# A recurrence's closing addition on GpSimd, and the turned maxima read by ScalarE

## The chip, the cores and the metric

One core of one Trainium2 chip runs the whole program. The time is device microseconds of one launch. The kernel before took 487.45 us, the median of three runs (486.83 to 490.58).

## The reference, cut to what matters

x is 2 x 1024 tokens of 128 channels. A layer norm gives xn, and the output is x plus two branches of xn.

```
xn  = layernorm(x)
out = x + attn_ref(xn) + ffn_ref(xn)

attn_ref(x):                       # a WKV recurrence over the 1024 tokens, per channel
    h = LN(x); k, v, r = mixes of h and h shifted, times w_tk, w_tv, w_tr
    y = wkv(decay, first, k, v)    # running max, running sum, running weighted sum
    x1 = x + sigmoid(r) * y
    h2 = LN(x1); ck, cr = mixes of h2 and h2 shifted
    return x1 + sigmoid(cr @ w_cr) * (square(relu(ck @ w_ck)) @ w_cv)

ffn_ref(x):                        # 16 heads of width 8, weights from a gated sum of experts
    q, k, v = effective weights applied to x
    ctx = softmax(q k^T, over keys) v
    return ctx @ w_o + b_o
```

The last line of `attn_ref` has the addition that the change moves. The maxima are those of the softmax in `ffn_ref`: each query's largest score over its 1024 keys.

## The kernel before, in words

**Attention.** There are 32 attention rows (2 batches x 16 heads), taken as 16 pairs of heads. For each pair the scores are made twice. First with queries on the partitions, only to find the row maxima: 32 "places" of 128 queries x 512 keys, each one bf16 matmul (`fill_place`, L1256) into one of three PSUM banks in turn (5, 6, 7), which VectorE reduces to one negated maximum per query (`read_place`, L1080). The two halves of a row are combined at the pair's last place (L1084). A 33rd place, `TURN_PLACE`, is a TensorE transpose of these 128 x 16 maxima (L1250) into 16 x 128 in the next bank of the same three; VectorE copies it to `max_rows` in SBUF (L1075). GpSimd splits it into three bf16 parts (`split_max`, L616 to L622), and SyncE writes these as three more rows of the queries (`place_max`, L448, six DMAs).

Then the scores are made again with keys on the partitions, maxima subtracted by those extra rows (`scores`, L1330), into banks 0 to 3. ScalarE takes the exponential of 2 x 512 columns at a time (`exps`, L887), and TensorE multiplies them by the values into bank 4 (`values`, L1341). A pair has 8 steps of 128 keys, each with two such exponentials.

**The order.** The program is unrolled over 16 pairs x 8 steps. Every engine has its own list in program order, and semaphores join them. In each step TensorE issues: two places of a later pair, the step's scores (half h = 0, then h = 1), two more places, the transposed maxima if it is their turn, the values of the step before, then perhaps a product of the recurrence. VectorE reads the step's four places in order, then the recurrence's operations of that step (`branch`). ScalarE does the two exponentials, then its own `branch`. A place may be filled once the place three fills earlier has been read; the semaphore `a_read` counts all reads, the transposed ones too.

**The recurrence.** The other branch is spread over the same steps, in four quarters of 256 tokens. A quarter lasts four pairs, 32 steps, and step t of a quarter has fixed work: windows are copied by GpSimd at t = 1, three scans run on VectorE at t = 2, 6 and 12, ScalarE has a Relu and an Exp at each of t = 9 to 12, the second layer norm and mixes come at t = 17 to 21, and the products at t = 22 to 29 (`PRODUCT_STEP`). At t = 29 VectorE multiplies the product by the gate into `gx` (L1061) and adds `x1` into `RT` (L1063), with `rt_ready`. GpSimd's copy of the quarter's ends at the next t = 1 (L639) waits for `rt_ready`, and so does TensorE's last stage. The lists of GpSimd add the output bias to x at t = 30 (L694).

The transposed maxima of the next pair come at the fourth step after a pair's start: t = 4, 12, 20 and 28 of a quarter, 15 times in the loop, and once more before the loop, where ScalarE copies twelve `parts` (L776) of the second batch's queries and keys.

The places for a pair run about one and a half pairs ahead, so in the last quarter they end before t = 20.

Of the kernel before, what the change touches and what calls it, by code (L numbers as in the profile page):

```python
# [6 lines left out]
P = 128  # L7
TILES = B * T // P
CHUNK = 512
CHUNKS = B * T // CHUNK  # L10
HEADS, HD = 16, 8
EXPERTS, RANK, GATE_H = 8, 16, 32
PAIRS = B * HEADS // 2
KEY_TILES = T // P
PARTS = 3
# [7 lines left out]
TURN_PLACE = 4  # L23
SPLIT_STEP = 4
A_PLACES = 33
PV_BANK, A_BANK = 4, 5
# [4 lines left out]
SETS = 4  # L31
QUARTERS, QT = 4, 256
# [15 lines left out]
def build(nc, x, cols, mats, rows, gw1, gb1, gw2, gb2, out):  # L48
    F32, BF16 = mybir.dt.float32, mybir.dt.bfloat16
    ALU, ACT, AX = mybir.AluOpType, mybir.ActivationFunctionType, mybir.AxisListType  # L50

    ctx = ExitStack()
    with ctx:
# [3 lines left out]
        def sem(name):  # L57
            return ctx.enter_context(nc.semaphore(name))
# [16 lines left out]
        RT = sb("RT", [P, B, T])  # L75
# [70 lines left out]
        gated = sem("gated")  # L146
        relu_ready = sem("relu_ready")
        a_read = sem("a_read")
        max_parts_ready = sem("max_parts_ready")
        ctx_copied = sem("ctx_copied")  # L150
        moe_in = sem("moe_in")
# [139 lines left out]
        def bank(i):  # L291
            return banks[:, i, :]
# [46 lines left out]
        def exists(it, pair, k):  # L339


            n = it * SETS + pair
            if not isinstance(n, int):
                return True
            return 1 <= n <= PAIRS if k == TURN_PLACE else n < PAIRS

        def a_count(it, pair, k):

            n = it * SETS + pair
            if isinstance(n, int) and n == 0:  # L350
                return k if k < TURN_PLACE else k - 1
            if isinstance(n, int) and n == PAIRS:
                return PAIRS * A_PLACES - 1
            return n * A_PLACES + k - 1

        turns, place_turns = [], []
        for t in range(SETS * KEY_TILES):  # L360
            here = []
# [16 lines left out]
        def turn_bank(turn):  # L378
            return bank(A_BANK + (turn + A_PLACES + LEAD - 1) % 3)
# [7 lines left out]
        def wait_for_bank(pe, it, turn):  # L387

            if turn < 3:
                pe.wait_ge(a_read, a_count(it, *turns[turn]) - 1)  # L390
                return
            turn -= 3
            while isinstance(turns[turn], tuple) and not exists(it, *turns[turn]):
                turn -= 3
            if isinstance(turns[turn], tuple):
                pe.wait_ge(a_read, a_count(it, *turns[turn]) + 1)
            else:
                taken, of, n = taken_by[turns[turn]]
                pe.wait_ge(taken, it * of + n)
# [11 lines left out]
        def first(p):  # L411
            return isinstance(p, int) and p == 0
# [118 lines left out]
        def _(pool):  # L531
# [77 lines left out]
            def split_max(p, s, it=0, pair=0):  # L609
                rows_, res_ = max_rows[:, s % 2, :], max_res[:, s % 2, :]  # L610
                m0, m1, m2 = (max_parts[:, s % 2, i, :] for i in range(PARTS))
                transposed = a_count(it, pair + 1, TURN_PLACE) + 1
                pool.wait_ge(a_read, transposed)
                if not (isinstance(p, int) and p < 2):
                    pool.wait_ge(b_ready, (p - 1) * 16 + 1)
                g.tensor_tensor(m0, rows_, zero_rows[:, :], ALU.add).then_inc(max_part, 1)  # L616
                pool.wait_ge(max_part, p * 3 + 1)
                g.tensor_tensor(res_, rows_, m0, ALU.subtract).then_inc(max_part, 1)
                pool.wait_ge(max_part, p * 3 + 2)
                g.tensor_tensor(m1, res_, zero_rows[:, :], ALU.add).then_inc(max_part, 1)  # L620
                pool.wait_ge(max_part, p * 3 + 3)
                g.tensor_tensor(m2, res_, m1, ALU.subtract).then_inc(max_parts_ready, 1)  # L622
# [10 lines left out]
            def branch(t, q):  # L633
# [56 lines left out]
                        mix(q, i, h2[:, :, 0:QT])  # L690
                if t == 30:

                    here = x_sb[:, 4 * q:4 * q + 4, :]
                    g.tensor_tensor(here, here, vb_ob[:, 1:2, :].to_broadcast([P, 4, C]), ALU.add  # L694
                                    ).then_inc(xob_ready, 1)
# [25 lines left out]
        def _(act):  # L721
# [61 lines left out]
            for u, n in enumerate(CHUNK_ORDER):  # L783
                act.wait_ge(h_transposed, u + 1)
                a.activation(hT[:, n // 2, 1 + CHUNK * (n % 2):1 + CHUNK * (n % 2 + 1)], bank(h_bank(u)), ACT.Identity,
                             bias=col("ln1_b"), scale=col("ln1_g")).then_inc(h_ready, 1)

            def keep_v(n):

                act.wait_ge(v_ps, n + 1)  # L790
                here = V[:, 8 * (n // 2):8 * (n // 2) + 8, 4 * (n % 2):4 * (n % 2) + 4, :]
                a.copy(here.rearrange("p r k w -> p k r w"), bank(v_bank(n)).rearrange(
                    "p (k r w) -> p k r w", k=CHUNK // P, w=2 * HD)).then_inc(v_read, 1)
# [29 lines left out]
            keep_v(3)  # L823
            keep_kvr(2)
            keep_kvr(3)
            for i in range(PARTS):
                for j in range(CHUNKS):
                    part(j, 1, i)

# [2 lines left out]
            def branch(t, q):  # L832
# [47 lines left out]
                if t == 28:  # L880
                    act.wait_ge(cr_step, q * 2 + 2)
                    a.activation(ecr[:, :, :], ecr[:, :, :], ACT.Exp, scale=-1.0).then_inc(cr_ready, 1)

            def exps(p, step):
                for h in range(2):
                    act.wait_ge(b_ready, p * 16 + 2 * step + h + 1)
                    a.activation(probs[:, (2 * step + h) % 4, :, :], banks[:, 2 * h:2 * h + 2, :],  # L887
                                 ACT.Exp).then_inc(b_read, 1)
# [5 lines left out]

            def head(p, j, it):
                exps(p, 0)
                if not first(p):
                    copy_ctx(p - 1, (j - 1) % SETS, it * 2 + (j - 1) // 2)
                branch(j * KEY_TILES, it)

            def rest(p, j, it):
                for step in range(1, KEY_TILES):
                    exps(p, step)
                    branch(j * KEY_TILES + step, it)

            def tail():
# [14 lines left out]
        def _(dve):  # L921
# [119 lines left out]
            def branch(t, q):  # L1041

                if t == 2:

                    dve.wait_ge(carried, q + 1)
                    dve.wait_ge(windows, q * 4 + 1)
                    scan(q, run_max, k_q, col("decay"), ALU.max, ALU.add, run_max_ready)
                if t == 6:

                    dve.wait_ge(decays_ready, q * 2 + 2)  # L1050
                    scan(q, run_sum, w1, w2, ALU.mult, ALU.add, sum_ready)
                if t == 12:
                    dve.wait_ge(ev_ready, q + 1)
                    scan(q, run_acc, lo_u, ev, ALU.mult, ALU.add, acc_ready)
                if t == PRODUCT_STEP["mean"]:
                    dve.wait_ge(mean2_ps, q + 1)
                    v.tensor_tensor(flat(xc2), flat(x1), product_bank("mean"), ALU.subtract).then_inc(centred2, 1)
                if t == PRODUCT_STEP["cv"]:
                    dve.wait_ge(cr_ready, q + 1)
                    dve.wait_ge(cv_ps, q + 1)  # L1060
                    v.tensor_tensor(flat(gx), product_bank("cv"), flat(ecr), ALU.mult).then_inc(gated, 1)  # L1061
                    dve.wait_ge(gated, q + 1)
                    v.tensor_tensor(RT[:, :, bass.ds(q * QT, QT)], x1[:, :, :], gx[:, :, :], ALU.add  # L1063
                    ).then_inc(rt_ready, 1)

            def read_place(it, pair, k, src):

                if not exists(it, pair, k):
                    return
                n, s, pair_n = a_count(it, pair, k), pair % 2, it * SETS + pair  # L1070
                if k == TURN_PLACE:
                    if not isinstance(pair_n, int) or pair_n >= 2:
                        dve.wait_ge(max_parts_ready, pair_n - 1)
                    dve.wait_ge(a_ready, n + 1)
                    v.tensor_copy(max_rows[:, (s + 1) % 2, :], src[0:2 * KEY_TILES, 0:P]).then_inc(a_read, 1)  # L1075
                    return
                e, c, h = place_of(k)
                u = 16 * e + 2 * c + h
                dve.wait_ge(a_ready, n + 1)
                v.tensor_reduce(neg_half[:, s, u:u + 1], src, axis=AX.X, op=ALU.max, negate=True  # L1080
                ).then_inc(a_read, 1)
                if k == A_PLACES - 1:
                    dve.wait_ge(a_read, n + 1)
                    v.tensor_reduce(neg_max[:, s, :], neg_half[:, s, :].rearrange("p (c h) -> p c h", h=2),  # L1084
                                    axis=AX.X, op=ALU.min).then_inc(half_combined, 1)

# [35 lines left out]
        def _(pe):  # L1122
# [155 lines left out]
            for pair, k in places(0, A_PLACES + LEAD):  # L1278
                if not exists(0, pair, k):
                    continue  # L1280
                n = a_count(0, pair, k)
                if n >= 3:
                    pe.wait_ge(a_read, n - 2)
                fill_place(0, pair, k, bank(A_BANK + n % 3))
                between(n)
            for j in range(CHUNKS):
# [148 lines left out]
```

## Time and profile before

| | before |
|---|---|
| median of three runs | 487.45 us |
| the profiled execution's own time | 487.07 us |
| its span, first to last instruction | 485.3 us |
| TensorE matmul busy | 443.6 us, 91% |
| VectorE busy | 372.2 us, 77% |
| ScalarE busy | 354.2 us, 73% |
| GpSimd busy | 180.9 us, 37% |
| chain that ended last, by engine | PE 58%, DVE 23%, ACT 13% |
| granted TensorE clock, mean | 0.981 |

The loop's first scores start at 76.8 us and its last exponential at 463.1 us. In the trace's names PE is TensorE, PEld its weight loads, DVE VectorE, ACT ScalarE, POOL GpSimd, SPq SyncE's DMA queue. A row of the timeline merges equal instructions (x4) and gives their common stretch; in square brackets stands the idle time of the engine before it and what ended it.

### The profile page before, as it was taken

The page shows a single profiled execution, that of the slowest core. Times are in us where ns is not written, and L with a number is a line of the kernel's source. Part 1 is how long each engine was busy: PE and PEld are TensorE (multiplying, and loading weights), DVE is VectorE, ACT ScalarE, POOL GpSimd, SP SyncE. Part 2 cuts the span into 40 slices and gives each one's busy share as a digit, 9 for nine tenths or more (in the row PEclk, how much of TensorE's full clock was granted, in tenths as well). Part 3 has the DMA queues.
Part 4 walks back from the last instruction along what each step waited for, and adds up shares of the span by engine and source line. Part 5 has one row for each costly group of instructions (what it writes and reads, how often), then busy time and mean ns, then how long its engine had stood idle before and what let it go on. Part 6 is the DMA issues. An engine that isn't in the chain of part 4 may idle for free.

```text
span 485.3 us, 8374 instructions
## 1 busy us (share of the span) xinstructions
PE 443.6 (91%) x3156; PEld 147.9 (30%) x3158; DVE 372.2 (77%) x670; ACT 354.2 (73%) x453; POOL 180.9 (37%) x236
## 2 busy tenths in 40 slices
PE   2886998999999999999999999999999999989996
PEld 2751322222223322222232222222322222222275
DVE  7543997999988689999877899998778999940113
ACT  2266773689888666898986668989875689899651
POOL 7048940414651414146514141375141313751200
PEclk9999995999999999999999999999999999999998
DMA  6004421132323223323232232332322321102132
GB/s 219 11 8 52 61 23 23 12 54 26 57 22 59 19 45 33 51 28 56 23 58 22 28 51 50 30 52 26 57 24 22 55 45 12 28 9 80 31 105 91
DMA packets 46684, 21.35 MB, mean 44 GB/s; under 512 B 37556, under 2 KB 37684, under 8 KB 46644
## 3 DMA queue, kind: packets, MB, share of 16 engines
q1 hardware_dynamic: 45824, 20.13, 25.5%
q10 hardware_dynamic: 820, 0.68, 0.4%
q8 instruction: 25, 0.41, 0.3%
q14 instruction: 15, 0.12, 0.1%
HBM read 4.88 MB, written 5.24 MB: 21 GB/s over the span
## 4 chain that ended last, share of the span: by engine, by line
PE 58%; DVE 23%; ACT 13%; issue 2%; SPq 2%; DMA 1%; DVEq 0%
PE banks L1341 17%; DVE neg_half L1080 15%; PE banks L1330 12%; PE banks L1256 11%; ACT probs L887 9%; PE banks L1302 8%; DVE run L1038 3%; PE banks L1231 2%; PE banks L1164 2%; PE banks L1388 2%; PE banks L1383 2%; PE banks L1129 1%; ACT work L846 1%; SPq L431 1%; ACT work L844 1%
## 5 line engine op out<-in xcount | busy, mean ns | idle before, releaser
L1080 DVE TENSOR_REDUCE neg_half<-banks 128x1 f32<-128x512 f32 x512 | 319.1, 682 | 39.1 <-PE banks L1256 37.4
L887 ACT ACTIVATE probs<-banks 128x1024 f32<-128x1024 f32 x256 | 247.7, 1022 | 66.3 <-PE banks L1330 63.6
L1341 PE MATMUL banks<-probs,v_op 128*32 128x512 f32 x1024 | 137.2, 608 | 0.4 <-ACT probs L887 0.4
L1256 PE MATMUL banks<-k_main,q_main 64*128 64x512 bf16 x512 | 120.3, 388 | 15.0 <-DVE neg_half L1080 12.1
L1330 PE MATMUL banks<-q_main,k_main 64*128 64x512 bf16 x512 | 101.2, 382 | 5.0 <-ACT probs L887 3.7
L1330 PE MATMUL banks<-q_tail,k_tail 35*128 35x512 bf16 x512 | 100.9, 381 | 0.0
L1256 PEld LDWEIGHTS banks<-k_main,q_main 64*128 64x128 bf16 x512 | 36.0, 94 | 168.1 <-DVE neg_half L1080 145.2
L1330 PEld LDWEIGHTS banks<-q_main,k_main 64*128 64x128 bf16 x512 | 26.0, 95 | 44.5 <-ACT probs L887 32.1
L1330 PEld LDWEIGHTS banks<-q_tail,k_tail 35*128 35x128 bf16 x512 | 26.6, 95 | 23.7 <-issue 1.1
L1061 DVE TENSOR_TENSOR rec<-banks,quarter_in 128x512 f32<-128x512 f32 x4 | 2.8, 690 | 37.8 <-PE banks L1302 37.8
L700 POOL TENSOR_TENSOR work<-work 128x512 f32<-128x512 f32 x12 | 12.5, 1040 | 49.8 <-ACT work L872 49.8
L1341 PEld LDWEIGHTS banks<-probs,v_op 128*32 128x32 f32 x1024 | 20.2, 108 | 33.1 <-issue 30.0
L616 POOL TENSOR_TENSOR max_parts<-max_rows,zero_rows 16x128 bf16<-16x128 f32 x16 | 11.2, 701 | 31.9 <-DVE max_rows L1075 31.9
L649 POOL TENSOR_TENSOR xn_tok<-run 128x512 f32<-128x512 f32 x4 | 4.2, 1039 | 49.7 <-DVE run L1038 49.7
L1302 PE MATMUL banks<-xn_tok,mat_sb 128*32 128x512 f32 x160 | 20.8, 592 | 0.0
L654 POOL TENSOR_TENSOR work<-work 128x512 f32<-128x512 f32 x4 | 5.1, 1276 | 41.8 <-ACT work L840 41.8
L1129 PE MATMUL banks<-ones_c,xn_tok 128*128 128x1 f32 x32 | 7.2, 353 | 8.8 <-DVE xn_tok L929 8.8
L658 POOL TENSOR_TENSOR hT<-work,quarter_in 128x512 f32<-128x512 f32 x4 | 5.1, 1272 | 18.7 <-ACT work L846 18.7
L1231 PE MATMUL banks<-work,mat_sb 128*128 128x512 f32 x16 | 8.9, 639 | 3.1 <-POOL work L594 2.8
L872 ACT ACTIVATE work<-banks 128x512 f32<-128x512 f32 x12 | 7.2, 601 | 5.7 <-PE banks L1302 5.7
L1302 PE MATMUL banks<-work,mat_sb 128*32 128x512 f32 x96 | 11.0, 592 | 0.0
L776 ACT ACTIVATE parts<-banks,qb_s 128x512 bf16<-128x512 f32 x9 | 6.1, 686 | 6.6 <-PE banks L1164 5.7
(164 smaller groups left out, 429.4 us busy)
## 6 DMA issues: line engine op xcount, KB each, us to landing
ctx_dram<-ctx_sb SPq DMA_DIRECT2D x16, 256.0 KB, 2.0
q_main<-parts SPq DMA_DIRECT2D x64, 48.0 KB
k_main<-parts SPq DMA_DIRECT2D x64, 48.0 KB
parts<-ctx_dram SPq DMA_DIRECT2D x8, 256.0 KB, 4.4
mat_sb<-in_mats_dram SPq DMA_DIRECT2D x2, 768.0 KB, 5.3
q_tail<-max_parts SPq DMA_DIRECT2D x96, 2.0 KB
q_main<-parts SPq DMA_DIRECT2D x32, 32.0 KB
k_main<-parts SPq DMA_DIRECT2D x32, 32.0 KB
```

The costliest lines, as they stand in the source:

```text
L616: g.tensor_tensor(m0, rows_, zero_rows[:, :], ALU.add).then_inc(max_part, 1)
L700: g.tensor_tensor(kk[i][:, :, :], kk[i][:, :, :], kk[i][:, :, :], ALU.mult).then_inc(kk_ready, 1)
L887: a.activation(probs[:, (2 * step + h) % 4, :, :], banks[:, 2 * h:2 * h + 2, :], ACT.Exp).then_inc(b_read, 1)
L1038: v.tensor_tensor_scan(out_[:, b, 1:], c0[:, b, :], data1, out_[:, b, 0:1], op0, op1).then_inc(done, 1)
L1080: v.tensor_reduce(neg_half[:, s, u:u + 1], src, axis=AX.X, op=ALU.max, negate=True).then_inc(a_read, 1)
L1129: last = mm(banks[:, 4, 24 + b:25 + b], xn_tok[:, i, :], ones_c[:, :], start=(k == 0), stop=(k == TILES // B - 1))
L1164: mm(bank(j), w_eff[:, t, b, :], columns_of(xnT, n), start=True, stop=True).then_inc(left_ps[j], 1)
L1231: mm(bank(kvr_bank(m)), mat("t" + "kvr"[m % 3]), mix_slot[m % MIX_SLOTS], start=True, stop=True).then_inc(kvr_ps, 1)
L1256: mm(dst, q_main[HALF * e:HALF * (e + 1), s, P * c:P * c + P], k_main[HALF * e:HALF * (e + 1), s, CHUNK * h:CHUNK * h + CHUNK], start=True ...
L1302: last = mm(dst[g:g + 32, :], weights[:, g:g + 32], moving, start=start, stop=stop)
L1330: last = mm(bank(2 * h + e), k_rows[HALF * e:HALF * e + used, at, P * step:P * step + P], q_rows[HALF * e:HALF * e + used, at, CHUNK * h:C ...
L1341: last = mm(banks[g:g + 32, PV_BANK, :], v_op[:, s % 2, step, e, :], probs[:, (2 * step + h) % 4, e, :], start=(step == 0), stop=(step == ...
```

## The change

The addition into `RT` leaves VectorE's step 29 for the head of GpSimd's step 30. The copy of the transposed maxima leaves VectorE's `read_place` for ScalarE: `copy_turned`, called behind the step's two exponentials and ahead of ScalarE's `branch` of that step. The reads of that place get a semaphore of their own, `turn_read`, and `read_of` says for each fill which semaphore and count stand for its read. Before the loop ScalarE copies the first transposed maxima between the first four and the last eight `parts`.

```diff
+        turn_read = sem("turn_read")
...
+        fill_seq = [(n, k) for n in range(PAIRS + 1) for k in range(A_PLACES) if exists(0, n, k)]
+
+        def read_of(at):
+
+            n, k = fill_seq[at]
+            turned = sum(place[1] == TURN_PLACE for place in fill_seq[:at + 1])
+            return (turn_read, turned) if k == TURN_PLACE else (a_read, at + 1 - turned)
...
             def split_max(p, s, it=0, pair=0):
-                transposed = a_count(it, pair + 1, TURN_PLACE) + 1
-                pool.wait_ge(a_read, transposed)
+                pool.wait_ge(turn_read, p + 1)
...
                 if t == 30:
 
+                    pool.wait_ge(gated, q + 1)
+                    g.tensor_tensor(RT[:, :, bass.ds(q * QT, QT)], x1[:, :, :], gx[:, :, :], ALU.add
+                                    ).then_inc(rt_ready, 1)
                     here = x_sb[:, 4 * q:4 * q + 4, :]
...
+            def copy_turned(n, src):
+
+                if n >= 2:
+                    act.wait_ge(max_parts_ready, n - 1)
+                act.wait_ge(a_ready, fill_seq.index((n, TURN_PLACE)) + 1)
+                a.copy(max_rows[:, (n + 1) % 2, :], src[0:2 * KEY_TILES, 0:P]).then_inc(turn_read, 1)
...
-            for i in range(PARTS):
+            for j in range(CHUNKS):
+                part(j, 1, 0)
+            copy_turned(1, bank(A_BANK + fill_seq.index((1, TURN_PLACE)) % 3))
+            for i in (1, 2):
                 for j in range(CHUNKS):
                     part(j, 1, i)
...
+            def turned_step(p, j, it, step):
+
+                for turn in (*place_turns[j * KEY_TILES + step][0], *place_turns[j * KEY_TILES + step][1]):
+                    pair, k = turns[turn]
+                    if k == TURN_PLACE and exists(it, pair, k):
+                        copy_turned(it * SETS + pair, turn_bank(turn))
...
                     exps(p, step)
+                    turned_step(p, j, it, step)
                     branch(j * KEY_TILES + step, it)
...
                     v.tensor_tensor(flat(gx), product_bank("cv"), flat(ecr), ALU.mult).then_inc(gated, 1)
-                    dve.wait_ge(gated, q + 1)
-                    v.tensor_tensor(RT[:, :, bass.ds(q * QT, QT)], x1[:, :, :], gx[:, :, :], ALU.add
-                    ).then_inc(rt_ready, 1)
...
                 if k == TURN_PLACE:
-                    if not isinstance(pair_n, int) or pair_n >= 2:
-                        dve.wait_ge(max_parts_ready, pair_n - 1)
-                    dve.wait_ge(a_ready, n + 1)
-                    v.tensor_copy(max_rows[:, (s + 1) % 2, :], src[0:2 * KEY_TILES, 0:P]).then_inc(a_read, 1)
                     return
```

TensorE's waits for a free bank (`wait_for_bank`, and the loop ahead of the main one) name `read_of` of the same fill as before.

## Rows read from the trace of the kernel before

**Rows 1.** Stretches by `windows`: busy us (instructions) by engine, then PEclk, DMA share, GB/s.
```profile
74.00:85.00 11.00, 9.74 (x41) 2.79 (x42) 7.78 (x14) 3.88 (x4) 0.00 (x0) 0.53 0.22 25
167.30:264.90 97.60, 93.36 (x736) 26.81 (x732) 86.51 (x146) 77.64 (x94) 35.91 (x44) 1.00 0.28 39
```

**Rows 2.** Groups of instructions by shape: busy us, mean ns, idle before.
```profile
L893 ACT COPY ctx_sb<-banks 128x512 f32<-128x512 f32 x16 | 9.5, 592 | 1.2 <-PE banks L1341 1.2
...
L694 POOL TENSOR_TENSOR x_sb<-x_sb,vb_ob 128x512 f32<-128x512 f32 x4 | 5.1, 1269 | 0.0
...
L1063 DVE TENSOR_TENSOR RT<-work,rec 128x512 f32<-128x512 f32 x4 | 2.8, 691 | 0.1
...
L769 ACT ACTIVATE mat_sb<-mat_sb 128x128 f32<-128x128 f32 x1 | 0.3, 312 | 0.0
```

**Rows 3.** Chain of waits (start, length, what) about step 29 of the second quarter.
```profile
268.42 0.70 DVE rec L1061
...
269.15 0.69 DVE RT L1063
...
270.50 0.39 PE banks L1256
```

**Rows 4.** VectorE's timeline (start, length, instruction) at step 17 of that quarter.
```profile
228.39 0.69 DVE L1057 TENSOR_TENSOR work<-work,banks 128x512 f32<-128x512 f32 x1 [0.76 <-PE banks L1302]
228.99 2.48 DVE L1080 TENSOR_REDUCE neg_half<-banks 128x1 f32<-128x512 f32 x4
```

**Rows 5.** GpSimd's timeline, step 2 of the third quarter.
```profile
283.96 1.04 POOL L649 TENSOR_TENSOR xn_tok<-run 128x512 f32<-128x512 f32 x1 [11.62 <-DVE run L1038]
```

**Rows 6.** VectorE's row reduction, line 1080, one line's view: ns min/median/max.
```profile
L1080 DVE TENSOR_REDUCE neg_half<-banks x512: 653/680/693, 42.2 to 429.4; 128x1 f32<-128x512 f32 x171
```

**Rows 7.** VectorE's timeline behind the copy of step 4.
```profile
191.74 0.69 DVE L1080 TENSOR_REDUCE neg_half<-banks 128x1 f32<-128x512 f32 x1 [0.30 <-PE banks L1256]
```

**Rows 8.** ScalarE's timeline, the exponentials of steps 5 and 29.
```profile
192.18 1.02 ACT L887 ACTIVATE probs<-banks 128x1024 f32<-128x1024 f32 x1 [1.16 <-PE banks L1330]
...
263.16 1.94 ACT L887 ACTIVATE probs<-banks 128x1024 f32<-128x1024 f32 x2 [0.51 <-PE banks L1330]
```

**Rows 9.** Chain of waits at step 12, and ScalarE's copy at step 8.
```profile
202.77 0.48 ACT ctx_sb L893
...
213.82 0.19 DVE max_rows L1075
```

**Rows 10.** ScalarE's timeline, the exponentials of step 13.
```profile
215.89 1.92 ACT L887 ACTIVATE probs<-banks 128x1024 f32<-128x1024 f32 x2
```

**Rows 11.** TensorE's weight loads and matmuls at step 14.
```profile
217.86 0.10 PEld L1330 LDWEIGHTS banks<-q_main,k_main 64*128 64x128 bf16 x2 [0.28 <-ACT probs L887]
...
217.92 0.38 PE L1330 MATMUL banks<-q_main,k_main 64*128 64x512 bf16 x2
...
218.35 0.46 PE L1256 MATMUL banks<-k_main,q_main 64*128 64x512 bf16 x2
```

**Rows 12.** TensorE's weight loads at step 22.
```profile
240.84 0.10 PEld L1330 LDWEIGHTS banks<-q_main,k_main 64*128 64x128 bf16 x2 [0.54 <-ACT probs L887]
```

**Rows 13.** The path of the maxima from step 12 to 16: GpSimd, SyncE's queue, TensorE.
```profile
214.08 1.47 POOL L616 TENSOR_TENSOR max_parts<-max_rows,zero_rows 16x128 bf16<-16x128 f32 x1 [2.95 <-DVE max_rows L1075]
...
L616 POOL TENSOR_TENSOR max_parts<-max_rows,zero_rows x16: 442/444/1473, 69.6 to 432.2; 16x128 bf16<-16x128 f32 x16
...
217.09 4.00 SPq L448 DMA_DIRECT2D q_tail<-max_parts  x6
...
222.46 0.38 PE L1330 MATMUL banks<-q_main,k_main 64*128 64x512 bf16 x2
```

**Rows 14.** Before the loop: chain of waits, and two matmuls of TensorE's timeline.
```profile
69.23 0.19 DVE max_rows L1075
...
68.09 0.28 PE L1250 MATMUL banks<-ident,neg_max 128*16 128x128 f32 x1
...
69.65 0.39 PE L1170 MATMUL banks<-parts,neg_ident 128*128 128x512 bf16 x1
```

More of the change, by code:

```diff
@@ L389, in wait_for_bank @@
             if turn < 3:
-                pe.wait_ge(a_read, a_count(it, *turns[turn]) - 1)
+                pe.wait_ge(*read_of(a_count(it, *turns[turn]) - 2))
                 return
@@ L395, in wait_for_bank @@
             if isinstance(turns[turn], tuple):
-                pe.wait_ge(a_read, a_count(it, *turns[turn]) + 1)
+                pe.wait_ge(*read_of(a_count(it, *turns[turn])))
             else:
@@ L896, in head @@
                 exps(p, 0)
+                turned_step(p, j, it, 0)
                 if not first(p):
@@ L1082, in read_place @@
                 if k == A_PLACES - 1:
-                    dve.wait_ge(a_read, n + 1)
+                    dve.wait_ge(*read_of(n))
                     v.tensor_reduce(neg_max[:, s, :], neg_half[:, s, :].rearrange("p (c h) -> p c h", h=2),
@@ L1282, in _ @@
                 if n >= 3:
-                    pe.wait_ge(a_read, n - 2)
+                    pe.wait_ge(*read_of(n - 3))
                 fill_place(0, pair, k, bank(A_BANK + n % 3))
```

## The prediction

> **What bounds the kernel.** I began with the stretches [rows 1]. Quarters repeat every 97.6 us at full clock. In one TensorE is busy 93.4 us, VectorE 86.5, ScalarE 77.6, GpSimd 35.9. No engine is full, so each moved operation must be followed in the chain of waits. In most steps it goes through TensorE alone. It goes through VectorE where the recurrence puts something between the reads of places, and through ScalarE where a branch stands between exponentials. An edit counts only there.
>
> **The addition into RT, off VectorE.** The multiply by the gate starts at 268.42, the addition at 269.15, and TensorE's next place, waiting for the first read behind them, starts at 270.50 [rows 3]: all on the chain. Without it that read follows the multiply directly. A tensor_tensor from PSUM is followed by a read after 0.60 [rows 4], so the read starts at 269.02 and not at 269.15 + 0.60 = 269.75: 0.73 us sooner. VectorE's reads of that step and the next two stand back to back, so they carry it to the next quarter. Three quarters have places behind step 29; in the last one there is nothing left to read and TensorE's last stage comes later. Gain 3 x 0.73 = 2.19 us.
>
> **The addition, on GpSimd.** GpSimd takes 1.27 us for two full operands [rows 2], against 0.69 on VectorE. Its step 30 now waits for `gated`; behind it are queued the bias addition (another 1.27), the quarter's ends and four windows. What hides them: GpSimd sits idle 11.6 us before step 2's scan is done [rows 5], and the scan needs only the ends and the first window. In the last quarter the bias addition is needed by VectorE's last stage, after the exponentials have ended. I price it at nothing; without the cover it would cost 1.27 a quarter. The Trainium skill ("SBUF — State Buffer", Terms, shared port pair) speaks against the move: the two engines lock each other out of a shared port for a whole instruction. What that would do to the reads here is priced among the rivals.
>
> **The copies, off VectorE.** There are 16, each worth 0.19 in the chain [rows 9]. At steps 4, 20 and 28 (11 of the 15 in the loop) VectorE then idles for TensorE's next place 0.30 at one [rows 7], the others alike (behind the last quarter's step 20 no read follows at all): no gain. At step 12 (4 times) the copy stands before the scan on the chain [rows 9]: 0.19 each. Before the loop it also stands on it [rows 14]: 0.19 once.
>
> **The copies, on ScalarE.** No row shows a 16x128 copy there. Durations: 592 ns for 128x512 out of PSUM, 312 for 128x128 in SBUF [rows 2]. What counts is what it holds up: the 592 ns copy takes 0.48 in the chain [rows 9], 0.11 less, as the next starts before it ends. From 0.31 this makes 0.20, which I take, since the size is the same. Bounds: 0.08 (0.19, VectorE's pitch for it, less 0.11) and 0.59, a whole large copy with nothing overlapped. Call it C. The Trainium skill ("VectorE: DVE Perf Modes", the TRN2 errata) has another: 172 cycles plus one per element at 1.2 GHz for ScalarE from PSUM, so an estimated 0.25 long and 0.14 held up; the rule gives 0.57 for the 512 copy, near the row's 0.592. By it the sum below would be 1.7 us faster than before.
>
> Where is C exposed?
> - Steps 4 and 28: ScalarE idles 1.16 and 0.51 before the next exponentials [rows 8]. Hidden. TensorE needs the bank only a step later.
> - Step 12: ScalarE has no gap. The exponentials of step 13 run 215.89 to 217.81 and TensorE's load for the second half of step 14 waits for them until 217.86 [rows 10, 11]; the matmul at 217.92 is just not late. Pushed by C they end at 217.81 + C, the matmul comes 0.05 to 0.07 later: 218.08 with C = 0.20, so 0.16 late. The two places behind it take 0.46 instead of 0.38 [rows 11], since the second waits 0.08 for the read of this step's first place; a late first half absorbs that. Net C - 0.11 = +0.09, which replaces the 0.19 gained at VectorE: if C were 0 the step would give back -0.19.
> - Step 20: no gap at ScalarE either, its layer-norm and mix operations run end to end with exponentials, and TensorE's load at step 22 already waits for them [rows 12]. C in full, +0.20.
> - Before the loop: four `parts` now wait for the transpose at 68.09 (0.28) and C: the first then ends at 68.37 + 0.05 + 0.20 + 0.69 = 69.31, and TensorE takes it at 69.65 [rows 14]. Hidden by 0.34.
>
> Both exposed steps come in all four quarters.
>
> **The new wait and the maxima's path.** GpSimd's split at step 12 starts 0.9 us later than before (behind 214.6 instead of 213.8), but its first operation took 1.47 us there beside VectorE's scan, against a median of 0.44 [rows 13], and the scan is then nearly over: it ends at about the same time. By the Trainium skill's port rule, above, the row is as it should be, since the scan reads SBUF. The six DMAs are issued until 221.09 and step 16 scores at 222.46 [rows 13]: 1.4 us in which they must land. This is the tightest point; I cost it at nothing, and bound it at +-0.3 a quarter.
>
> **The sum**, against the profiled execution's own 487.07 us (span 485.3 and 1.8 around it):
> - RT: -2.19
> - before the loop: -0.19
> - step 12: 4 x 0.09 = +0.36
> - step 20: 4 x 0.20 = +0.80
>
> Together -1.22: 485.85. The median of the three runs lies 0.38 above this execution, so I forecast **486.2 us**, 0.25% faster. As a formula, with all else as above: -2.82 + 8C. Net zero is at C = 0.35.
>
> **The rivals.**
> - *ScalarE pays more* (0.14). The mechanism is the copy's length at steps 12 and 20. If its wait and its semaphore leave nothing overlapped, C passes 0.35 and the kernel is slower; at C = 0.59 it is +1.90, 489.35. For it: ScalarE has no gap at either place. Against: every ScalarE row that I read overlaps by 0.1.
> - *RT's gain doesn't arrive* (0.09). Something else, the fill of `gated`'s bank or the exponentials, ends that wait. Then -0.63 + 1.60 (8C) = about +1.0: 488.4. Against it: ScalarE idles there, and the second place of step 30 waits for nothing but the read.
> - *GpSimd's addition blocks VectorE's reads* (0.03). Instead of -0.73 it would be +0.54 a quarter: 3 x 1.27 on top of the sum, 490.0. Against it: all 512 reads took 653 to 693 ns [rows 6], whatever GpSimd did beside them.
> - *The clock's low stretch moves* (0.08). From 74 to 85 us the granted clock was 0.53 [rows 1], near the 1.2 GHz level, after TensorE had been waiting on reads; all else in the loop ran at 2.4 GHz. The edit shifts the reads just ahead of it by 0.2 us. In such 11 us the matmul work of 9.74 us would take about half at full clock, less what waits anyway: I take 3.3 us either way, 482.9 or 489.5, 0.04 each.
> - *The maxima land late at step 16* (0.04): 4 x 0.3 on top, 487.4.
> - The forecast case has 0.62. That the change doesn't do what it says I can leave out: both moves are plain edits of the lists.
>
> **Range and chances.** The forecast case by itself spans C from 0.08 to 0.3, 485.1 to 487.0, and runs of this kernel differ by 0.6 to 3.1 us. The range 484.6 to 489.0 takes in the rivals but the clock's two ends and the blocked reads. Within 1% (4.9 us, about what a measurement tells from no change) lie all cases but tails of the clock: faster by over 1% 0.03, within 1% 0.94, slower 0.03.
>
> **What would show it.** `RT` on GpSimd right behind the gate multiply, 1.27 long, and TensorE's place of step 30 at 0.73 less after that multiply's start (1.35 instead of 2.08). A quarter of 97.6 - 0.73 + 0.09 + 0.20 = 97.2 us. ScalarE's copy at 0.25 to 0.31 long; the load at step 14 waiting longer than 0.28, the load at step 22 longer than 0.54. No idle TensorE before step 16. It would be wrong if quarters lengthened, if GpSimd's first split operation at step 12 still took 1.4 us, or if the low clock lasted other than about 10 us.

## The result and the profile after

| | before | after |
|---|---|---|
| median of 20 runs each, side by side | 488.95 us | 485.87 us |
| lowest and highest run | 485.51 to 491.61 | 482.72 to 489.30 |
| profiled execution's own time, span | 487.07, 485.3 | 484.93, 483.2 |
| a quarter (step 29's last product to the next) | 97.61, 97.60 | 96.82, 96.83 |

After to before is 0.9948, 95% interval 0.9923 to 0.9972: faster by 0.5%, 1.4 to 3.8 us. The forecast was 486.2, 1.22 us less than before. The spans of the two profiled executions differ by 2.1 us. By the starts of the step-29 multiply, the changed kernel is 0.22 behind in the first quarter (171.04 to 170.82), and then 0.56, 1.33 and 2.12 ahead (457.68 to 459.80): three times 0.77 to 0.79, less 0.22. Single runs of either kernel differ by more than the change brings, so what follows is read by quarters, which repeat to 0.03 us.

The chain of waits of the changed kernel about step 29 of the second quarter (start, length, what):

```profile
267.86 0.69 DVE rec L1091
268.56 0.61 DVE neg_half L1103
...
269.21 0.39 PE banks L1279
```

Against [rows 3]: the read now follows the gate multiply by 0.70 and TensorE's place starts 1.35 after that multiply, where it was 2.08. That is the forecast number, 1.35.

GpSimd's timeline at the same place, and then VectorE's scan of step 2 that it must not delay:

```profile
268.63 1.27 POOL L702 TENSOR_TENSOR RT<-work,rec 128x512 f32<-128x512 f32 x1 [4.90 <-DVE rec L1091]
...
271.23 0.62 POOL L650 COPY quarter_in<-kept_k 128x512 f32<-128x512 f32 x1
```
```profile
281.20 1.38 DVE L1068 TENSOR_TENSOR_SCAN run<-quarter_in,run,col_sb 128x256 f32<-128x256 f32 x2
```

The addition takes 1.27 and the first window starts at 271.23, 10 us before the scan, which waits for nothing (no bracket).

ScalarE's timeline at steps 12 and 20:

```profile
212.28 1.92 ACT L915 ACTIVATE probs<-banks 128x1024 f32<-128x1024 f32 x2
214.09 0.24 ACT L804 COPY max_rows<-banks 16x128 f32<-16x128 f32 x1
214.24 0.72 ACT L865 ACTIVATE hT<-work,neg_first 128x512 f32<-128x512 f32 x1
```
```profile
236.95 0.24 ACT L804 COPY max_rows<-banks 16x128 f32<-16x128 f32 x1
237.09 1.33 ACT L888 ACTIVATE xn_tok<-xn_tok,col_sb 128x512 f32<-128x512 f32 x2
```

The copy is 0.24 long and holds up what is behind it by 0.15 (214.09 to 214.24) and 0.14 (236.95 to 237.09). I had taken 0.20 from the nearest rows; the Trainium skill's figure ("VectorE: DVE Perf Modes", the TRN2 errata) gave an estimated 0.25 and 0.14, and the trace agrees with it.

TensorE's timeline at step 17, before and after:

```profile
226.21 1.07 PE L1341 MATMUL banks<-probs,v_op 128*32 128x512 f32 x8
227.26 1.06 PE L1302 MATMUL banks<-work,mean_w 128*32 128x512 f32 x8
```
```profile
225.71 1.06 PE L1364 MATMUL banks<-probs,v_op 128*32 128x512 f32 x8
226.59 1.06 PE L1325 MATMUL banks<-work,mean_w 128*32 128x512 f32 x8
```

Here is what I had not foreseen. The product of the means started 1.05 us after the values ahead of it; now it does so after 0.88, which is what the eight matmuls of values ahead of it take when nothing waits. So before the change it was held for 0.17. What held it shows in the timelines of TensorE's weight loads, GpSimd and VectorE (its row is that of the stretch from 226 to 227 us), first before, then after:

```profile
227.23 0.19 PEld L1302 LDWEIGHTS banks<-work,mean_w 128*32 128x32 f32 x8 [0.87 <-DVE neg_half L1080]
...
225.85 1.27 POOL L676 TENSOR_TENSOR work<-hT,quarter_in 128x512 f32<-128x512 f32 x1
...
225.75 1.88 DVE L1080 TENSOR_REDUCE neg_half<-banks 128x1 f32<-128x512 f32 x3
```
```profile
226.56 0.19 PEld L1325 LDWEIGHTS banks<-work,mean_w 128*32 128x32 f32 x8 [0.69 <-DVE neg_half L1103]
...
225.17 1.28 POOL L684 TENSOR_TENSOR work<-hT,quarter_in 128x512 f32<-128x512 f32 x1
```

The product waits for two things: its PSUM bank, which is free once VectorE has read the second of the step's four places, and its operand `x1`, which GpSimd's last addition of step 16 writes (`x1_ready`). The bracket names VectorE. But the read of that second place, the first of the three in the row, starts at 225.75 and takes 0.68, so the bank was free 0.8 us before the load of 227.23. `x1` was ready at 227.12, 0.11 before it. In every quarter of all ten traces the product's first load starts 0.11 to 0.12 after `x1` is written. So it was GpSimd's `x1` that held TensorE, not a bank.

TensorE's weight loads at steps 21 and 22 of the changed kernel, against [rows 12]:

```profile
240.28 0.10 PEld L1353 LDWEIGHTS banks<-q_main,k_main 64*128 64x128 bf16 x2 [0.65 <-ACT probs L915]
```

The wait for the exponentials grew from 0.54 to 0.65: step 20's copy costs 0.11. The same wait at step 14 grew from 0.28 to 0.60, as the prediction's signs had it.

### The profile page after: what moved, and what is told of

Its sections match the earlier page's. It is cut to its first block, busy times and chain, and to the rows that moved or that the text cites. A ratio compares the mean times of both kernels' runs of the same rounds, so it can differ in the third digit from the quotient of the medians.

```text
span 483.2 us, 8374 instructions
## 1 busy us (share of the span) xinstructions
PE 444.6 (92%) x3156; PEld 147.4 (31%) x3158; DVE 367.2 (76%) x650; ACT 356.0 (74%) x469; POOL 182.1 (38%) x240
## 3 DMA queue, kind: packets, MB, share of 16 engines
q1 hardware_dynamic: 45824, 20.13, 25.5%
## 4 chain that ended last, share of the span: by engine, by line
PE 54%; ACT 22%; DVE 18%; issue 2%; SPq 2%; DMA 1%; DVEq 0%
PE banks L1364 15%; ACT probs L915 14%; DVE neg_half L1103 12%; PE banks L1353 11%; PE banks L1279 10%; PE banks L1325 8%; PE banks L1254 2%; DVE run L1068 2%; PE banks L1411 2%; PE banks L1406 2%; PE banks L1187 1%; ACT work L867 1%; ACT work L865 1%; PE banks L1152 1%; ACT xn_tok L888 1%
## 5 line engine op out<-in xcount | busy, mean ns | idle before, releaser
L624 POOL TENSOR_TENSOR max_parts<-max_rows,zero_rows 16x128 bf16<-16x128 f32 x16 | 7.1, 446 | 36.0 <-ACT max_rows L804 36.0
L1254 PE MATMUL banks<-work,mat_sb 128*128 128x512 f32 x16 | 10.7, 775 | 2.8 <-POOL work L603 2.8
L702 POOL TENSOR_TENSOR RT<-work,rec 128x512 f32<-128x512 f32 x4 | 5.1, 1273 | 21.4 <-DVE rec L1091 21.4
L666 POOL TENSOR_TENSOR hT<-work,quarter_in 128x512 f32<-128x512 f32 x4 | 5.1, 1273 | 18.7 <-ACT work L867 18.7
```

The source lines that it names most:

```text
L1254: mm(bank(kvr_bank(m)), mat("t" + "kvr"[m % 3]), mix_slot[m % MIX_SLOTS], start=True, stop=True).then_inc(kvr_ps, 1)
```

## The experiments

A quarter is the time between the starts of step 29's last product in the first and second quarter, read from each trace. Three of these kernels and the changed one were also timed on one chip beside the kernel before (488.70 us, 35 runs). The other four ran once each, so only their quarters are read.

| kernel | quarter | expected | median of 12 runs, or the one run | to before (95%) |
|---|---|---|---|---|
| before | 97.61 | | 488.70 (35 runs) | |
| changed | 96.80 | 96.83 | 485.01 | 0.9944 (0.9912 to 0.9976) |
| addition only | 96.86 | 96.88 | 488.11 | 0.9980 (0.9941 to 1.0019) |
| copies only | 97.53 | 97.55 | 486.55 | 0.9992 (0.9956 to 1.0028) |
| ScalarE copies at step 12 only | 96.69 | 96.72 | 484.01 | 0.9914 (0.9880 to 0.9948) |
| ScalarE copies but at step 12 | 97.00 | 96.99 | 485.21 (one) | |
| each copy three times | 97.43 | 97.43 | 485.10 (one) | |
| addition nine times | 101.27 | 97.8 | 507.81 (one) | |
| addition five times | 96.83 | 96.8 | 486.26 (one) | |

**The changed kernel again.** No edit.

> The changed kernel again, on the chip of its parts. A quarter was 97.60 us before and 96.83 in its first profile. My account of that: the addition gives -0.72 at step 29, the copy off VectorE gives -0.17 at step 17 (not at step 12, where I had placed it), ScalarE's copy costs +0.01 at step 12 and +0.11 at step 20. Expected: a quarter of 96.83 again, and a time 0.3 to 0.6% under the kernel before. If instead the gain of 2.5 us in the medians is mostly drift between chips, the ratio is above 0.9975.

96.80 and 96.80 us a quarter, 0.56% faster. The gain repeats on another set of runs.

**The addition alone.** The copies stay on VectorE:

```diff
# kernel before
-                    dve.wait_ge(gated, q + 1)
-                    v.tensor_tensor(RT[:, :, bass.ds(q * QT, QT)], x1[:, :, :], gx[:, :, :], ALU.add
-                    ).then_inc(rt_ready, 1)
...
                 if t == 30:
+                    pool.wait_ge(gated, q + 1)
+                    g.tensor_tensor(RT[:, :, bass.ds(q * QT, QT)], x1[:, :, :], gx[:, :, :], ALU.add
+                                    ).then_inc(rt_ready, 1)
```

> Only the addition on GpSimd; the copies stay on VectorE. Theory (the parts add): a quarter of 97.60 - 0.72 = 96.88 us, no change at steps 12 to 22, three quarters of them 2.2 us in all. Rival (the gain at step 29 needs the copies gone too, because VectorE's backlog is one thing): a quarter above 97.1.

The quarter is 96.86, 0.75 less than before. Its chain of waits at step 29:

```profile
271.97 0.69 DVE rec L1064
272.66 0.61 DVE neg_half L1080
...
273.32 0.39 PE banks L1256
```

The place starts 1.35 after the multiply here too, so the addition's gain stands by itself and the rival falls. Its median is 0.6 us under that of the kernel before. The interval (0.9941 to 1.0019) takes in the 2.2 us of the quarters as well as no gain at all, so the whole times don't show it; the section on the hardware has the likely reason.

**The copies alone.** The reverse: the changed kernel with the addition back behind the multiply.

```diff
# changed kernel
                     v.tensor_tensor(flat(gx), product_bank("cv"), flat(ecr), ALU.mult).then_inc(gated, 1)
+                    dve.wait_ge(gated, q + 1)
+                    v.tensor_tensor(RT[:, :, bass.ds(q * QT, QT)], x1[:, :, :], gx[:, :, :], ALU.add
+                    ).then_inc(rt_ready, 1)
```

> Only the copies on ScalarE; the addition stays on VectorE. Theory: a quarter of 97.60 - 0.17 + 0.01 + 0.11 = 97.55 us, so the time is that of the kernel before within 0.1%. Rival, my prediction's own account (VectorE's 0.19 lost at step 12, ScalarE's copy exposed there and in full at step 20): 97.60 + 0.05 + 0.15 = 97.8 us with the copy's measured 0.15.

97.53: the copies gain 0.08 a quarter, where my prediction's account has them lose. The two parts add: 0.75 + 0.08 = 0.83 against the 0.79 to 0.81 of both together.

**VectorE copies at step 12 again.** The pair number n of the maxima picks the engine:

```diff
+        def on_scalar(n):
+            return n % 4 != 3
...
             def copy_turned(n, src):
+                if not on_scalar(n):
+                    return
...
                 if k == TURN_PLACE:
+                    if on_scalar(pair_n):
+                        return
+                    if pair_n >= 2:
+                        dve.wait_ge(max_parts_ready, pair_n - 1)
+                    dve.wait_ge(a_ready, n + 1)
+                    v.tensor_copy(max_rows[:, (s + 1) % 2, :], src[0:2 * KEY_TILES, 0:P]).then_inc(turn_read, 1)
                     return
```

> The changed kernel, but VectorE copies the maxima of step 12 again, ScalarE the others. Theory (the 0.19 us of that copy stays in VectorE's queue through its back-to-back reads and comes out where the product of step 17 waits for a bank): the product of step 17 starts 1.05 us after the values before it, as in the kernel before, and not 0.88; a quarter of 96.83 + 0.17 - 0.01 = 96.99 us. Rival (that 0.17 comes from something else, as the addition's move or the other copies): 0.88 stays and a quarter is 96.8.

TensorE's timeline at step 17:

```profile
225.50 1.06 PE L1376 MATMUL banks<-probs,v_op 128*32 128x512 f32 x8
226.56 1.07 PE L1337 MATMUL banks<-work,mean_w 128*32 128x512 f32 x8
```

The product starts 1.06 after the values again and the quarter is 97.00, 0.17 above the changed kernel's. With one copy back, step 17 loses its gain. So the 0.17 us come from the copy of step 12, five steps earlier. The expectation above has them travel in VectorE's queue. The traces show another way. TensorE's timeline at steps 13 and 14, before and after (the first half of step 14's scores starts at 217.48 and 216.79, the second at 217.92 [rows 11] and 217.50):

```profile
215.94 0.39 PE L1256 MATMUL banks<-k_main,q_main 64*128 64x512 bf16 x1 [0.35 <-DVE neg_half L1080]
...
217.48 0.38 PE L1330 MATMUL banks<-q_main,k_main 64*128 64x512 bf16 x2
```
```profile
215.25 0.39 PE L1279 MATMUL banks<-k_main,q_main 64*128 64x512 bf16 x1 [0.17 <-DVE neg_half L1103]
...
216.79 0.38 PE L1353 MATMUL banks<-q_main,k_main 64*128 64x512 bf16 x2
...
217.50 0.39 PE L1353 MATMUL banks<-q_main,k_main 64*128 64x512 bf16 x2
```

1. VectorE's queue is 0.19 shorter, and the place of step 13 waits 0.17 for its read instead of 0.35. The first half of step 14's scores comes 0.18 sooner.
2. TensorE's own list loses this at once. The second half of step 14 starts 0.71 behind the first instead of 0.44, since ScalarE's exponentials of step 13 end later by its copy; the two places behind it give 0.08 back (0.38 instead of 0.46).
3. Another path leaves from that first half: ScalarE's exponentials of step 14 and the logarithm behind them (L850), and GpSimd's operations from L666 on, which wait for that logarithm and end with `x1`. Before the change ScalarE was idle for 0.31 ahead of those exponentials, waiting for the scores, and that has room for the copy. This path keeps the 0.18.
4. At step 17 the product waits for `x1`, and there TensorE gets it.

GpSimd's first operation on that path, before and after:

```profile
220.65 1.28 POOL L666 TENSOR_TENSOR hT<-hT,quarter_in 128x512 f32<-128x512 f32 x1 [1.13 <-ACT hT L850]
```
```profile
219.96 1.28 POOL L674 TENSOR_TENSOR hT<-hT,quarter_in 128x512 f32<-128x512 f32 x1 [1.12 <-ACT hT L871]
```

GpSimd sits idle for 1.13 ahead of it in both, so an earlier split of the maxima isn't what brings `x1` forward. From the first half of step 14's scores to the product of the means it is 9.78 us in the three traces where VectorE copies at step 12, and 9.80 to 9.81 in the six where ScalarE does so once. VectorE's lead doesn't last: its last read of step 17 ends 1.41 after the start of the values before the change and 1.42 after it. No experiment delays this path alone; it is read from the times of all the traces.

**ScalarE copies at step 12 only.** The same edit with `n % 4 == 3`.

> The changed kernel, but ScalarE copies only the maxima of step 12; those of steps 4, 20 and 28 and the one before the loop are VectorE's again. Theory: VectorE has idle time behind those three, and step 20 no longer costs 0.11: a quarter of 96.72 us, 0.4 us in all, under what the times can tell. Rival (each copy that VectorE keeps costs its 0.19 somewhere later, as at step 12): a quarter of 96.83 - 0.11 + 3 x 0.19 = 97.3 us.

96.69 a quarter, 0.11 under the changed kernel, and not 97.3: the three other copies cost VectorE nothing. TensorE at step 22, where the stall grew by 0.11 in the changed kernel, starts the second half's matmuls here 0.42 behind the previous ones, as before; 240.28 in the changed kernel is 0.53 behind:

```profile
237.64 0.38 PE L1365 MATMUL banks<-q_tail,k_tail 35*128 35x512 bf16 x2
238.06 0.39 PE L1365 MATMUL banks<-q_main,k_main 64*128 64x512 bf16 x2
```
```profile
239.75 0.38 PE L1353 MATMUL banks<-q_tail,k_tail 35*128 35x512 bf16 x2
240.28 0.39 PE L1353 MATMUL banks<-q_main,k_main 64*128 64x512 bf16 x2 [0.15 <-ACT probs L915]
```

It is the fastest kernel of the study, at 0.9914 of the one before. Between it and the changed one only the quarters tell: 4 x 0.11 us is below what the runs resolve, and their intervals overlap.

**Each copy three times.** Two more go to a spare tile, in bf16:

```diff
                 act.wait_ge(a_ready, fill_seq.index((n, TURN_PLACE)) + 1)
+                for i in range(2):
+                    a.copy(spare_rows[:, i, :], src[0:2 * KEY_TILES, 0:P])
                 a.copy(max_rows[:, (n + 1) % 2, :], src[0:2 * KEY_TILES, 0:P]).then_inc(turn_read, 1)
```

> The changed kernel with each of ScalarE's copies made three times (two of them into a spare tile): 0.15 us more for each. Theory (ScalarE has no gap at steps 12 and 20 and has one at 4 and 28): +0.30 at step 12, +0.30 at step 20, nothing at 4 and 28, a quarter of 97.43 us; at that price, C = 0.45, the whole change would be near nothing. Rival (the copies sit in idle time everywhere and step 20's 0.11 has another cause): a quarter below 97.0. A second rival (the maxima's path is tight at step 16): TensorE idles before step 16's scores as well, and a quarter is above 97.6.

97.43. ScalarE at step 12, and behind the copies of step 4:

```profile
212.47 0.39 ACT L806 CAST spare_rows<-banks 16x128 bf16<-16x128 f32 x2
...
212.93 0.72 ACT L868 ACTIVATE hT<-work,neg_first 128x512 f32<-128x512 f32 x1
```
```profile
190.07 1.94 ACT L918 ACTIVATE probs<-banks 128x1024 f32<-128x1024 f32 x2 [0.72 <-PE banks L1356]
```

At step 12 the three hold up the branch by 0.46 (212.47 to 212.93); at step 4 ScalarE still idles behind them (the bracket of 190.07). So 0.30 more a copy costs 0.60 a quarter, at two of four steps, as the prediction's formula has it (2C). The maxima's path, 0.30 later as well, adds nothing. At this price the formula has the change lose 0.78 us, but the quarter is still 0.18 under the 97.61 of the kernel before: the gain of step 17 is what the formula lacks.

**The addition nine times**, and then **five times**, each waiting for the one before:

```diff
                     pool.wait_ge(gated, q + 1)
+                    for i in range(8):          # 4 in the second kernel, and 4 * q below
+                        g.tensor_tensor(RT[:, :, bass.ds(q * QT, QT)], x1[:, :, :], gx[:, :, :], ALU.add
+                                        ).then_inc(again, 1)
+                        pool.wait_ge(again, 8 * q + i + 1)
                     g.tensor_tensor(RT[:, :, bass.ds(q * QT, QT)], x1[:, :, :], gx[:, :, :], ALU.add
```

> The changed kernel with the addition made nine times on GpSimd, one after the other: eight more of about 1.3 us, 10.4 us. In the changed kernel GpSimd's first window is copied 9.4 us before VectorE's scan of step 2 starts. Theory (that gap is the cover, and GpSimd takes nothing from VectorE's reads beside it): the reads stay at 653 to 693 ns, and the scan starts about 1.0 us late in three quarters, so a quarter of 97.8 us. Rival (GpSimd's additions block or slow VectorE's reads): reads of 0.8 us or more beside them and a quarter over 100 us.

The quarter was 101.27, the next 100.22, far above the 97.8: the theory missed too. VectorE's timeline at step 2, TensorE's there, and the granted clock by stretches (PEclk is the third column from the end, ahead of the DMA share and GB/s):

```profile
188.77 1.94 DVE L1073 TENSOR_TENSOR_SCAN run<-quarter_in,run,col_sb 128x256 f32<-128x256 f32 x2 [1.44 <-POOL quarter_in L651]
```
```profile
191.35 0.60 PE L1284 MATMUL banks<-k_main,q_main 64*128 64x512 bf16 x1 [2.96 <-DVE neg_half L1108]
191.88 1.93 PE L1369 MATMUL banks<-probs,v_op 128*32 128x512 f32 x8
```
```profile
184.00:190.00 6.00, 4.39 (x39) 1.26 (x31) 4.56 (x8) 4.62 (x5) 5.84 (x8) 1.00 0.54 70
190.00:196.00 6.00, 4.65 (x21) 1.05 (x21) 4.56 (x8) 0.75 (x1) 4.39 (x5) 0.57 0.18 19
196.00:202.00 6.00, 6.00 (x45) 1.64 (x41) 4.72 (x8) 4.30 (x7) 1.72 (x4) 0.86 0.01 3
```

The scan waits 1.44 us for the window, near the 1.0 expected. Then three things come on top. GpSimd's last window copies run beside the scan, and both slow down: the scan pair takes 1.94 against 1.38, the copies 1.01 against 0.61. TensorE idles 2.96 us, where it idles 0.89 in the kernel before. And its granted clock falls to 0.57 for the next six microseconds, most of them at the level of 1.2 GHz: eight matmuls of values take 1.93 against 1.06 (225.71 above). The two later quarters repeat it, with 2.98 and 2.99 idle and a low clock behind them. All 512 of VectorE's reads took 658 to 693 ns, so the rival (blocked reads) falls although the time is near its own. What I left out were the slower scan and the low clock behind the idle time; that the one brings the other about is my reading of their order, no run tests it alone.

> The changed kernel with the addition made five times on GpSimd, four more of 1.35 us each with their waits, 5.4 us, which is inside the 9.4 us between GpSimd's first window and the scan of step 2. Theory (only a late scan costs time; nine additions were too many, and TensorE's clock fell on top): the quarter stays at 96.8 us, the scan of step 2 waits for nothing, no low clock in the loop after 90 us. Rival (each addition on GpSimd takes something from VectorE or TensorE beside it): half of the 3.4 to 4.4 us a quarter that eight more cost, a quarter of 98.5 to 99.

96.83, as the changed kernel, and the clock is 1.00 from 100 to 465 us; the second row is GpSimd's first window:

```profile
100.00:465.00 365.00, 348.83 (x2738) 97.49 (x2738) 290.73 (x478) 297.73 (x374) 155.20 (x176) 1.00 0.26 39
```
```profile
275.80 0.62 POOL L651 COPY quarter_in<-kept_k 128x512 f32<-128x512 f32 x1
```

Even with five additions the first window is copied 4 us before the scan at 280.38. In the loop one addition is covered several times over, and takes nothing from the engines beside it.

The last quarter has less cover. Nothing is left for VectorE to scan there, but TensorE's last stage needs `RT`. From the fourth quarter's multiply to the end it is 25.5 us in the kernel before and in the changed one, 27.6 with five additions and 33.0 with nine. The chain of waits with five:

```profile
461.69 1.27 POOL RT L704
...
463.00 1.31 POOLq L53
...
464.44 7.70 PE banks L1411 x32
```

In the changed kernel the addition ends at 459.73 and that stage starts at 463.15, 3.4 us later: one addition is free there too, four more are not.

## Why the prediction was right, and which terms were mis-sized

It named the sign, and the main term nearly to the hundredth. That 486.2 was forecast and 485.87 measured is in part luck. The kernel before has a median of 488.95 over 20 runs, 1.5 above the three that the forecast started from, and the gain was larger to match: 3.1 by the medians (1.4 to 3.8), 2.1 by the spans, where the forecast had 1.22. By its own steps, in us over the whole kernel:

| term | predicted | measured |
|---|---|---|
| RT off VectorE, 3 quarters | -2.19 | -2.2 (3 x 0.72 to 0.75) |
| the addition on GpSimd | 0 | 0 |
| copy before the loop | -0.19 | about 0 |
| first scores to the scan of step 2 | 0 | +0.30 |
| step 12, 4 times | +0.36 | -0.7 (0.17 at step 17) |
| step 20, 4 times | +0.80 | +0.44 |
| sum | -1.22 | -2.2 (-2.1 in the spans) |

- **RT**: right, by the addition-only kernel.
- **GpSimd's cover**: right. Four more additions still fit in the loop; in the last quarter 3.4 us cover the one.
- **Step 12** is the step that failed. The prediction said that the late exponentials *replace* the 0.19 gained at VectorE. For TensorE's own list they do: from the values that it issues in step 12 to those in step 14 it is 6.12 before and 6.13 after. But that gain had already brought step 14's first scores forward by 0.18, and a second path from there, through ScalarE's logarithm and GpSimd's `x1`, isn't touched by the late exponentials of step 13. It ends at the product of step 17, which TensorE issues and which waits for `x1`. I had followed the chain two steps past the copy and stopped; the row that would have said more is the 1.05 us before the product of step 17. That the 0.17 come from this copy is shown by putting it back; by which path, by the times.
- **C** was 0.15, not 0.20: 0.05 at each of eight places. At step 20 it cost 0.11, and why not the full 0.15 I can't say; the tripled copy costs its full length at both steps together.
- **First scores to the scan of step 2**: 10.50 before, 10.80 after, but 10.07 to 10.94 over all the traces, and the changed kernel alone shows 10.80 and 10.08: it belongs to the execution, not to the edit. A low stretch of the clock lies there (0.55 from 74 to 85 us in the first of these two, 0.69 in the second).
- **Before the loop**: the reads came no sooner, since there TensorE fills a place only every 0.64 us (at the same times before and after), between other matmuls, slower than VectorE's 0.60 a read. The chain named VectorE for the whole stretch, and I took its word for it:

```profile
69.97 0.39 PE L1279 MATMUL banks<-k_main,q_main 64*128 64x512 bf16 x1
...
70.61 0.39 PE L1279 MATMUL banks<-k_main,q_main 64*128 64x512 bf16 x1
```
```profile
66.84 9.17 DVE neg_half L1103 x15
```

  Fifteen reads in 9.17, as before: there, four, the copy and eleven took 2.39 + 0.19 + 6.59 = 9.17.
- **The rivals.** ScalarE pays more: its mechanism is real and its price was right (2C a quarter), but C is far from the point. The maxima late at step 16: GpSimd's first split operation takes 0.45 there now, and step 12's copies three times over didn't delay step 16. RT's gain missing and blocked reads: excluded. The clock's low stretch: it didn't move, 0.53 before and 0.55 after from 74 to 85 us.
- **The range** had two slips. By the formula the case C = 0.08 gives 485.3, not 485.1, and the first rival's end at C = 0.59 (489.35) lies outside 489.0.

## What to carry to other kernels

What an operation costs in an engine's list isn't settled where the chain of waits passes it. Find the first instruction that comes sooner without it, here the scores of step 14, and follow every path that leaves there until it meets the busiest engine again, not only that engine's own list. One path lost the gain after a step, another kept it for three.

The releaser that the profile names can be the wrong one where an instruction waits for several. Compare the end of each with the start of what waited: here 0.8 us against 0.11.

An added operation costs its own pitch (what it holds up the next one by) at each place where its engine has no gap, and nothing where it has one, so place it by the gaps: of four copies a quarter here, one was worth moving, two were indifferent and one was better left.

## What the runs showed of the hardware

**Runs differ ahead of the loop.** In the traces of this study the loop's first scores start at 75.2 to 80.6 us: 80.6 in the addition-only kernel, 75.2 in the one with tripled copies, though neither edit touches the stages ahead of 60 us. The granted clock in those stages differs (columns as in [rows 1]); first the kernel before, then the changed one, then the addition alone:

```profile
16.00:31.00 15.00, 12.99 (x45) 7.72 (x45) 8.01 (x31) 6.59 (x15) 4.03 (x4) 0.89 0.00 1
...
41.00:49.00 8.00, 5.47 (x16) 1.43 (x15) 4.47 (x8) 6.35 (x11) 6.34 (x7) 1.00 0.37 46
```
```profile
16.00:31.00 15.00, 12.66 (x53) 8.10 (x54) 9.58 (x33) 7.39 (x16) 4.04 (x4) 1.00 0.00 1
...
41.00:49.00 8.00, 6.44 (x15) 1.50 (x14) 4.57 (x8) 6.17 (x11) 7.17 (x7) 0.79 0.37 46
```
```profile
41.00:49.00 8.00, 5.27 (x12) 1.11 (x10) 2.58 (x4) 5.21 (x9) 6.34 (x7) 0.76 0.36 47
49.00:66.00 17.00, 16.64 (x58) 5.84 (x58) 14.18 (x22) 10.69 (x19) 14.09 (x23) 0.91 0.47 58
```

A low stretch falls now on the projections at 16 to 31 us, now on those near 45 us. Another lies between 74 and 100 us in every trace. From 100 to 465 us the clock is 1.00 in all but the kernel with nine additions. The traced execution of the addition-only kernel shows what this does to a whole time. It took 489.12 us against 487.07 of the kernel before, though from the loop's first scores to the last multiply by the gate it took 381.2 against 383.0: its loop began 3.8 us later. So I take the head to make most of the 3.5 to 6.6 us between single runs of one kernel, and to be why 12 runs of the addition alone show 0.6 us where its quarters show 2.2; for the runs without a trace this isn't shown. What decides where the low stretch falls stays open.

**A stall of TensorE can cost more than itself.** With nine additions TensorE idled for 2.96 to 2.99 us at step 2 in three quarters, and each time the granted clock was low just behind it (0.57 over six microseconds in the first). The window came 1.44 us late, and the quarters lengthened by 4.4, 3.4 and 4.4 us. With 0.89 us of idle time at the same place, the kernel before and the changed one show nothing of the kind: 1.00 from 100 to 465 us.

**GpSimd copies and VectorE scans slow each other** where they overlap (1.01 against 0.61 us, 1.94 against 1.38); its two-operand additions beside VectorE's reads of PSUM do not.
